# A decoder layer with a routed feed-forward: where GpSimd's and VectorE's small work stands, and one matmul for the two parts of W2

## What is computed

```python
x = x + attn(layernorm(x))          # over T, with squared distances as logits, 16 heads
x = x + xattn(layernorm(x), ctx)    # 16 heads, 64 context rows for each of 4 batches
x = x + ffn(layernorm(x))

def ffn(x):                         # E = 8 experts, F = 1024, k = 2048 / 8 = 256 rows each
    route_prob = softmax(xf @ Ws + bs, axis=-1).T
    route_vals, routes = top_k(route_prob, k)      # each expert takes its 256 best rows
    xin = xf[routes]
    h = gelu(einsum('ekd,edf->ekf', xin, W1) + b1[:, None, :])
    out = einsum('ekf,efd->ekd', h, W2) + b2[:, None, :]
    out = out * route_vals[..., None]
    return zeros.at[routes.reshape(-1)].add(out.reshape(-1, D))
```

## Time and profile before

| | us |
|---|---|
| median of 3 runs | 367.15 (365.62 to 367.66) |
| the profiled execution | 367.29 |
| its span, first to last instruction | 365.5 |

### The profile page before, as it was taken

How to read it: one execution, slowest core, us unless ns; L and a number is a source line. 1 busy time by engine, 2 the same in 40 slices (tenths; PEclk the granted TensorE clock), 3 DMA queues, 4 the chain that set the end, 5 groups by cost and what they waited for, 6 DMA issues and landing times.

```text
span 365.5 us, 6473 instructions
## 1 busy us (share of the span) xinstructions
PE 321.0 (88%) x2350; PEld 290.6 (79%) x2350; DVE 286.6 (78%) x637; ACT 189.5 (52%) x374; POOL 195.7 (54%) x248
## 2 busy tenths in 40 slices
PE   7989998899979999999999991126999999999991
PEld 7877886675559999999999881116999999999991
DVE  3888888858777888888888778778578699689860
ACT  2677655446464457657764643682417546652230
POOL 3778789723042537888788764605224515543222
PEclk9999999999989999999999996555999999999997
DMA  8950000000000135143331537301158757611222
GB/s 251 382 208 1 2 0 2 0 0 3 0 2 0 38 121 165 39 145 97 105 130 57 159 103 230 116 1 43 45 165 240 184 204 190 173 20 40 30 30 29
DMA packets 24047, 34.29 MB, mean 94 GB/s; under 512 B 1784, under 2 KB 20560, under 8 KB 23888
## 3 DMA queue, kind: packets, MB, share of 16 engines
q1 hardware_dynamic: 20112, 29.36, 24.6%
q0 software_dynamic: 3072, 4.20, 6.5%
q10 hardware_dynamic: 832, 0.32, 0.4%
HBM read 27.58 MB, written 6.29 MB: 93 GB/s over the span
## 4 chain that ended last, share of the span: by engine, by line
PE 73%; DVE 13%; POOL 6%; ACT 4%; issue 2%; POOLq 0%; DVEq 0%; ACTq 0%
PE bank L929 13%; PE bank L931 13%; PE bank L930 13%; PE bank L939 4%; PE q_banks L929 4%; PE q_banks L930 4%; PE q_banks L931 4%; DVE flags_all L1419 2%; PE bank L1593 2%; PE bank L778 2%; PE q_banks L723 2%; PE bank L741 2%; PE bank L757 2%; POOL acc L410 1%; PE bank L957 1%
## 5 line engine op out<-in xcount | busy, mean ns | idle before, releaser
L1718 POOL DMA_INDIRECT out_x<-ybuf,idx x16 | 26.0, 1628 | 59.8 <-DVE ybuf L1738 57.7
L1137 POOL TENSOR_TENSOR prob<-prob,rsum 128x1024 f32<-128x1024 f32 x15 | 28.6, 1905 | 17.3 <-DVE rsum L1245 17.3
L929 PE MATMUL bank<-W_hi,h_hi 128*128 128x256 f32 x128 | 37.2, 291 | 0.0
L929 PE MATMUL bank<-H_hi,PT_hi 128*128 128x256 f32 x128 | 36.5, 285 | 0.1
L931 PE MATMUL bank<-H_hi,PT_lo 128*128 128x256 f32 x128 | 36.3, 283 | 0.0
L930 PE MATMUL bank<-H_lo,PT_hi 128*128 128x256 f32 x128 | 36.2, 283 | 0.0
L931 PE MATMUL bank<-W_hi,h_lo 128*128 128x256 f32 x128 | 36.2, 283 | 0.0
L930 PE MATMUL bank<-W_lo,h_hi 128*128 128x256 f32 x128 | 36.2, 283 | 0.0
L1097 ACT ACTIVATE prob<-prob 128x1024 f32<-128x1024 f32 x16 | 16.9, 1059 | 34.7 <-DVE prob L1266 34.7
L1675 ACT ACTIVATE hbuf<-bank,b_cols 128x256 f32<-128x256 f32 x32 | 13.4, 471 | 40.1 <-PE bank L931 40.1
L1698 POOL DMA_INDIRECT xg<-xn_rows,idx x16 | 18.7, 1168 | 20.7 <-DVE idx L1766 16.4
(11 more groups left out here) (277 smaller groups left out, 1075.1 us busy)
## 6 DMA issues: line engine op xcount, KB each, us to landing
W_raw<-in_L_ffn_W SPq DMA_DIRECT2D x16, 1024.0 KB, 5.5
X<-in_x SPq DMA_DIRECT2D x4, 512.0 KB, 6.4
xn_rows<-xn SPq DMA_DIRECT2D x16, 128.0 KB, 1.7
out_x<-X SPq DMA_DIRECT2D x4, 512.0 KB, 3.7
Wq<-in_L_xattn_Wq SPq DMA_DIRECT2D x1, 1024.0 KB, 10.9
Wk<-in_L_xattn_Wk SPq DMA_DIRECT2D x1, 1024.0 KB, 13.8
Wv<-in_L_xattn_Wv SPq DMA_DIRECT2D x1, 1024.0 KB, 15.1
Wo<-in_L_xattn_Wo SPq DMA_DIRECT2D x1, 1024.0 KB, 17.1
```

What stands on the lines that cost most here:

```text
L929: t.matmul(out_ps, hi, rhs_hi, start=first, stop=False)
L1137: g.tensor_tensor(prob[:, s], prob[:, s], rsum[:, s].unsqueeze(2).to_broadcast([P, HX, CK]), ALU.mult).then_inc(prob_ready, 1)
L1718: g.indirect_dma_start(out_flat, bass.IndirectOffsetOnAxis(ap=idx[:, e, h:h + 1], axis=0), ybuf[:, h], None, bounds_check=last_row, oob_is ...
```

## The change

- The subtraction on `ws_sb` leaves VectorE's part 1 and becomes the last instruction of GpSimd's part 1.
- GpSimd's last weight half in `pool_drain` waits for `probs_ready`.
- VectorE copies the 60 trial values into PSUM ahead of the searches, and line 1419 reads them there.
- Part 4: `UNREAD` is 9. Ahead of expert 0 stand list 0, the unread products, the transposes of expert 0, then list 1. Lists 2 and 3 stand behind the 4th and the 8th chunk of its up product. On VectorE the one-hot of list 1 waits until GpSimd has issued the first gather (`first_asked`, a small memset behind it); `read_list(0)` and the splits of `vals` move ahead of it, `xgT_low(0)` ahead of `read_list(1)`.
- The two parts of W2 lie in one tile. For experts 0 to 6 the high part of h is multiplied with both in one matmul of 512 columns that fills a bank, the low part with the high one in a matmul of 256; VectorE then adds both halves of the bank, with one more instruction per half h. Expert 7 stays as it was.

```diff
+        W2_hi, W2_lo = W2[:, 0], W2[:, 1]
@@ pool_part1
             for j in range(NJ):
                 inverse_std(slice(j, NT, NJ), var2_ready, j + 1, rstd2_ready)
+            pool.wait_ge(cols_ready, 3)
+            g.tensor_tensor(ws_sb[:], ws_sb[:], gate_mean[:].unsqueeze(1).to_broadcast([P, MC, E]),
+                            ALU.subtract).then_inc(gate_ready, 1)
@@ dve_part1
             low_parts(3)
-            dve.wait_ge(cols_ready, 3)
-            v.tensor_tensor(ws_sb[:], ws_sb[:], gate_mean[:].unsqueeze(1).to_broadcast([P, MC, E]),
-                            ALU.subtract).then_inc(gate_ready, 1)
             statistics2(1)
@@ pool_drain
+            pool.wait_ge(probs_ready, 1)
             W_low(pool, LAST_HALVES[1])
@@ dve_part3
             v.memset(ones_f[:, 1, 0:1], 0.0)
+            trials = v3(banks[6][:, 0:4 * SEARCHES], SEARCHES)
+            order(v.tensor_copy(trials, trials_f[:]))
             dve.wait_ge(keysT_full, 1)
...
-                                                     in1=trials_f[:, r, b:b + 1].to_broadcast([P, P]), op0=ALU.subtract,
+                                                     in1=trials[:, r, b:b + 1].to_broadcast([P, P]), op0=ALU.subtract,
@@ pe_part4
-        UNREAD = 7
+        UNREAD = 9
+        LISTS_AT = {FC // 2 - 1: 2, FC - 1: 3}
...
             list_of(FIRST_LISTS[0])
-            list_of(FIRST_LISTS[1])
 
             for _ in range(UNREAD):
                 t.matmul(banks[2][:, 0:P], ident[:], ident[:], start=True, stop=True)
             transposes(EXPERTS[0])
-            list_of(FIRST_LISTS[2])
+            list_of(FIRST_LISTS[1])
...
-                        if e == 0 and f == FC // 2 - 1:
-                            list_of(FIRST_LISTS[3])
+                        if e == 0 and f in LISTS_AT:
+                            list_of(FIRST_LISTS[LISTS_AT[f]])
...
-                            mm = product3(banks[6 + h][:, 0:D], h_hi[:, f, hs], h_lo[:, f, hs], W2_hi[:, p, f], W2_lo[:, p, f],
-                                          f == 0, f == FC - 1)
+                            if e < E - 1:
+                                t.matmul(v3(banks[6 + h][:], 2), h_hi[:, f, hs], W2[:, :, p, f], start=f == 0, stop=False)
+                                mm = t.matmul(banks[6 + h][:, 0:D], h_lo[:, f, hs], W2_hi[:, p, f], start=False,
+                                              stop=f == FC - 1)
+                            else:
+                                mm = product3(banks[6 + h][:, 0:D], h_hi[:, f, hs], h_lo[:, f, hs], W2_hi[:, p, f],
+                                              W2_lo[:, p, f], f == 0, f == FC - 1)
@@ pool_part4
             gather(EXPERTS[0])
+            g.memset(asked[:], 0.0).then_inc(first_asked, 1)
             gather(EXPERTS[1])
@@ dve_part4
                     dve.wait_ge(down_full, NH * e + h + 1)
+                    if e < E - 1:
+                        order(v.scalar_tensor_tensor(out=ybuf[:, h], in0=banks[6 + h][:, D:2 * D],
+                                                     scalar=gates[:, e, h:h + 1], in1=ybuf[:, h], op0=ALU.mult,
+                                                     op1=ALU.add))
...
             onehot_of(FIRST_LISTS[0])
+            read_list(FIRST_LISTS[0])
             split_vals_by_position(1)
-            read_list(FIRST_LISTS[0])
+            split_vals_beside_pool(2, E, order)
+            dve.wait_ge(first_asked, 1)
             onehot_of(FIRST_LISTS[1])
+            xgT_low(EXPERTS[0])
             read_list(FIRST_LISTS[1])
-            split_vals_beside_pool(2, E, order)
             onehot_of(FIRST_LISTS[2])
             onehot_of(FIRST_LISTS[3])
-            xgT_low(EXPERTS[0])
             read_list(FIRST_LISTS[2])
             read_list(FIRST_LISTS[3])
```

More of the change, by code:

```diff
@@ L144, in build_program @@
         neg_half = region([("neg_half", [P, NT], F32)])
-        eps_col, warm = region([("eps_col", [P, 1], F32), ("warm", [P, 1], F32)])
+        eps_col, warm, asked = region([("eps_col", [P, 1], F32), ("warm", [P, 1], F32), ("asked", [P, 1], F32)])
         bias_cols, b1_cols = region([("bias_cols", [P, 3 * NC], F32), ("b1_cols", [P, E * FC], F32)])
@@ L176, in build_program @@
             [("beside1", [P, MC, 4, F], F32), ("W1_raw", [P, MC, 4, F], F32)])
-        (H_hi, H_lo), attn, (W2_hi, W2_lo), (_, W2_raw) = overlay(
+        (H_hi, H_lo), attn, (W2,), (_, W2_raw) = overlay(
             [("H_hi", [P, CB, NC, D], F32R), ("H_lo", [P, CB, NC, D], F32R)],
@@ L186, in build_program @@
              ("outb_bc", [P, D], F32), ("Wq", [P, MC, HK], F32)],
-            [("W2_hi", [P, 4, FC, D], F32R), ("W2_lo", [P, 4, FC, D], F32R)],
+            [("W2", [P, 2, 4, FC, D], F32R)],
             [("beside2", [P, 4, FC, D], F32), ("W2_raw", [P, 4, FC, D], F32)])
@@ L1549, in build_program @@
         added = sem("added")
+        first_asked = sem("first_asked")
         EXPERTS = [At(0, e, 2) for e in range(E)]
```

## The result

The changed kernel has a median of 372.48 us (4 runs, 371.21 to 377.64) against 366.44 for the kernel before (4 runs, 365.62 to 367.66). The ratio is 1.014, with an interval of 1.0102 to 1.0178: the change costs 3.7 to 6.5 us. Its profiled execution took 371.2 us with a span of 369.5, 4.0 us above the span of before. The forecast was 371.8.

The account below looks back on a forecast made before the run. TensorE bounds the second stage's start and the experts, with dependent work and VectorE's searches between. 4.55 + 1.6 - 2.2 - 0.15 + 2.05 - 1.35 = +4.5 on 367.3 gave 371.8 us, range 368.5 to 375.5.

Parts of the forecast that it names:

- wait at the gate, and clock: Start of second stage: TensorE waits for GpSimd's subtraction ahead of line 888, +4.55; lower granted clock behind the gap, +1.6.
- weight half behind the probabilities: End of second stage: line 1315 no longer runs beside GpSimd's weight half, -2.2 (bounds -2.3 and -2.0).
- search and ranks: VectorE's searches with the trial values in PSUM: -0.15 together (bounds -0.6 and +0.9).
- first gather: Ahead of expert 0: one-hot of list 1 no longer beside GpSimd's gather, so expert 0 starts earlier, -1.1.
- expert 0: list inside, h parts held, its share of part 5: Expert 0: one more list inside, +1.05; h parts start only behind list 3, +2.1; merged W2 matmuls save some.
- part 5 in the other experts: Down products: two 256-column matmuls become one of 512; -1.35 over experts 0 to 6, VectorE's additions cost 0.
- the low stretch near 105: TensorE's clock at 1.2 GHz from about 105.4 to 108.8 in the earlier trace; the same expected once more at the gap.
- I had this as a rival: Clock not lost at the new gap, or the stretch near 105 not coming a second time: 370.2, chance 0.15.
- The trials: Line 1419's 14 instructions freed from stretches, -0.55; line 1435 moved towards GpSimd's copies, +0.3; copy into PSUM, +0.1.
- Part 2: GpSimd's last weight half moved behind probs_ready, so line 1315 is short: -2.2.
- the rival with a second low stretch: Clock falls once more in expert 0's stall behind list 3: 373.4; chance 0.15, shared with no faster gather.

Follow-up runs that it names:

- the version with part 1 alone: The kernel before with only the subtraction on ws_sb moved to the end of GpSimd's first part: 373.1 us, ratio 1.0191.
- the one without it: The changed kernel with the subtraction on ws_sb back on VectorE: 366.14 us, ratio 0.9988 to the kernel before.
- the one with the wait at line 957's reader: The changed kernel, subtraction still on GpSimd, TensorE waiting for gate_ready only ahead of the first product that reads ws_sb: 366.21 us, ratio 0.9992.

## Why the prediction was right

The forecast was 371.8, and the sum +4.5 against a span that grew by 4.0. The places were right. That the sum came so close is in part luck: single terms are off by 0.4 and 0.9 one way and by 0.2 to 0.4 the other. Term by term, forecast and trace:

| step | forecast | trace |
|---|---|---|
| wait at the gate, and clock | +4.55 and +1.6 | +5.26 at the router |
| weight half behind the probabilities | -2.2 | -2.16 |
| search and ranks | -0.15 | -0.58 |
| first gather | -1.1 | -1.08, of which the gather 0.77 |
| expert 0: list inside, h parts held, its share of part 5 | +2.95 | +3.18 |
| part 5 in the other experts | -1.15 | -0.79 |
| behind the last scatter's issue | 0 | +0.2 |

- **The wait.** Right in place and size: the version with part 1 alone, the one without it, and the one with the wait at line 957's reader say the same from three sides. The gap less the old wait is 4.45, foreseen 4.55. In my sum the low stretch near 105 stays and a new one comes; here a new one came (1.5 us, foreseen 1.6) and the one near 105 did not, which gave 1.26 back. I had this as a rival. The 1.6 was lucky: in the four other executions with the idle gap the slower products cost 2.4 to 2.9, the dearest beyond my bound of 2.6. The low stretch near 105 is there in four of the eight profiled executions without the wait at line 890, and in none of the six with it. So the same orders run with it and without it, and whether the wait by itself removes it is open.
- **The weight half.** -2.2 was read from the earlier trace rows, and both the changed kernel and the version with the half put back have it to 0.1 where the search begins.
- **The trials.** The step that failed in its reason. The sum came out small, as forecast, but I let the stretches of the earlier trace rows stay with GpSimd's copies as if the search stood still. Part 2 moves the search by 2.2 us, GpSimd's copies wait for a DMA, and so they part by themselves. I saw that for line 1435 and priced it there (+0.3; measured 0.1, 0.45 against 0.35), and did not apply it to the fourteen. In its terms, the 26 instructions gave 0.68 and the one for `keys` took 0.1 more. What PSUM adds by itself is 0.004 us for each instruction saved, 0.1 in all, and the copy takes 0.06 of it. The Trainium skill's page "VectorE: DVE Perf Modes", in the section on the TRN2 errata, gives a PSUM source 62 cycles more than an SBUF one. The runs disagree for this instruction: 345 ns with the trials in PSUM, 349 and 350 with them in SBUF.
- **The gather.** The change of expert 0's start is right to 0.02, the reason only in part. The instruction took 2.10 beside the one-hot in five kernels and 1.33 away from it, so the gather itself gave 0.77 and not 1.1. I had not foreseen the 1.33; it is now beside the work on `vals_h`, and whether that is what lengthens it was not tested. The missing 0.3 came from TensorE, which before went from its unread products through the transposes without a wait for rows, so that it and not the gather set the start. I had named the new order of the unread products, but given it no price of its own. The Trainium skill's page "SBUF — State Buffer", section "Who interferes with whom", says that a VectorE instruction with two SBUF inputs contends with a GpSimd instruction that reads SBUF; the traces agree, 2.10 against 1.33. By the page's inference on descriptors the one-hot would not slow the gather; the experiment, 2.10 again with little else moved, speaks against that.
- **Expert 0.** The mechanism is the one forecast, the h parts behind list 3 and 4.5 us in a row, and undoing it gave 1.6 in the median (across two batches) and 2.3 in the trace (forecast 2.1). The clock did not fall in that hold in the changed kernel; in the experiment with the one-hot beside the gather it did, so the rival with a second low stretch was a real one.
- **Part 5.** Mis-sized: 0.06 to 0.20 an expert, 0.13 on the average, instead of 0.19. The down products themselves are longer than I had them. Those of experts 4, 5 and 6 took 5.63, 5.73 and 5.70 us, where I had 5.55 and before took 5.84. Why is open. It is not a wait for VectorE: of the idle time ahead of the 512-column matmuls, 1.2 us in all, 1.0 is one wait, for the first low part of h in expert 0. VectorE's fourteen new instructions, whose cost I set to 0 because the late h parts of experts 4 and 5 would catch up, made TensorE wait for nothing else of size.

## What to carry to other kernels

A wait belongs in front of the instruction that reads the tile, not in front of a stage: the same move of a 0.22 us instruction cost some 6 us with one wait and nothing that could be measured with the other. Moving one engine's work in time moves it against every engine that waits for something else, so two edits against the same stretch are not added until the order of events has been laid out anew. And starting a stage earlier by putting its side work inside of it is a trade: here the microsecond that expert 0 started earlier was paid back by the list.

## What the runs showed of the hardware that was not expected

- The same idle gap of 5.21 us ahead of the same 32 products costs a different amount of clock in each execution. The granted clock fell 0.4 us before the gap's end in the changed kernel (32 products in 5.14) and 2 us before it in the version with part 1 alone (6.05); in three more they took 6.14, 6.25 and 6.57, and with the gap filled 3.67.
- In the experiment with the one-hot beside the gather the low clock left over from the search outlasted the start of dense work: TensorE had waits of 0.41 and 0.66 us behind the unread products, and the clock stayed at 1.2 GHz until some 5 us into expert 0. A gather that was 0.8 us late went with 3.8 more on the mean time.
- The first gather's instruction took 1.33 or 2.10 us on GpSimd. It took 2.10 where a one-hot of 2048 columns had begun 0.32 us ahead of it (five kernels, the same 0.32 in each), and a later one 1.80 with a one-hot begun 0.28 ahead (258.91 and 258.63 in the changed kernel).
- The kernel before has two times, 2.1 us apart in their means (365.65 and 367.72), with no change of the program. That they differ by the low stretch near 105 is likely but not shown: the one trace of before is of the slower group and has it, and of the versions without the wait the four with the stretch have a mean granted clock of 0.943 to 0.949, the four without it 0.951 to 0.953.
